# Attention scores from split operands stacked by DMA, in a causal softplus attention with a feed-forward network

## The reference

```
q, k, v = split(x @ w_qkv.T);  k_y = x @ w_ky.T           # split into 16 heads
L, L_y  = q k^T / 4,  q k_y^T / 4                          # 512 x 512 each, causal
agg = sum(exp(clip(L_y, -15, 15)) * mask) + 1e-6
w   = softplus(log(|L| + 1e-6) - log(agg + 1e-6)) * mask
out = (w / (sum(w) + 1e-6)) @ v;   x = layernorm(x + out @ w_proj.T)
h = silu(x @ w1.T * s1) * (x @ w2.T * s2)
h = gelu(h @ h1.T * s3);  h = gelu(h @ h2.T * s4);  x = layernorm(x + h @ w3.T * s5)
```

## The kernel before

| beat | after `scores_y`, early | after `sum_exps` and `scores_w`, before `sum_weights` |
|---|---|---|
| 0 | `sum_values` | `turn` (even slot) |
| 1 | `flip_sums` | `ky_proj` for the next unit |
| 2 | `spread_c` | `turn` (even), `project_out` (odd) |
| 3 | `k_proj` | |
| 4 | `flip_sums` | `q_proj` for the next unit |
| 5 | `v_proj` | `project_out` (even) |

## Time and profile before

### The profile page before, as it was taken

One profiled execution on the slowest core, in us unless ns is written; L12 is line 12 of the kernel. 1 busy time (PEld: TensorE's weight loads), 2 busy tenths in 40 slices (PEclk: granted clock), 3 DMA queues, 4 the chain that ended last, 5 costly groups with the idle time before them and its releaser, 6 DMA issues.

```text
span 1367.8 us, 22887 instructions
## 1 busy us (share of the span) xinstructions
PE 1248.2 (91%) x8214; PEld 807.9 (59%) x8214; DVE 728.6 (53%) x1232; ACT 622.8 (46%) x819; POOL 138.2 (10%) x188
## 2 busy tenths in 40 slices
PE   4888999999999999875499999999999999999996
PEld 2433444444443444433388788787887878878785
DVE  2556778686877767675343534435244352443523
ACT  3666767767677766563232313223132231322311
POOL 1212122222221122220000000000000000000000
PEclk9999999999999999998799999999999999999998
DMA  2011312222321411000640000000000000000000
GB/s 90 1 55 32 97 60 96 73 92 77 101 83 46 138 46 55 1 31 32 230 180 16 31 0 16 31 15 31 0 15 31 15 31 0 15 31 15 31 0 16
DMA packets 31942, 66.88 MB, mean 49 GB/s; under 512 B 2848, under 2 KB 8608, under 8 KB 31904
## 3 DMA queue, kind: packets, MB, share of 16 engines
q1 hardware_dynamic: 31904, 66.35, 14.3%
HBM read 46.42 MB, written 19.92 MB: 49 GB/s over the span
## 4 chain that ended last, share of the span: by engine, by line
issue 51%; POOL 0%; DVE 0%; POOLq 0%; DVEq 0%
POOL f_rstd L865 0%; DVE f_res L872 0%; POOLq L965 0%; DVEq L877 0%; POOL f_minus_half L963 0%; POOLq L83 0%
## 5 line engine op out<-in xcount | busy, mean ns | idle before, releaser
L991 ACT ACTIVATE f_h_full<-f_layer_bank,f_scales 128x512 f32<-128x512 f32 x128 | 88.0, 687 | 354.7 <-PE f_layer_bank L1105 354.6
L380 ACT ACTIVATE e_ring<-score_banks 128x1024 f32<-128x1024 f32 (+1 forms) x192 | 158.8, 879 | 134.4 <-PE score_banks L704 134.2
L541 DVE TENSOR_TENSOR w_ring<-score_banks,keep 128x1024 int32<-128x1024 int32 (+1 forms) x192 | 191.8, 1041 | 48.5 <-PE score_banks L704 47.1
L1105 PE MATMUL f_layer_bank<-f_ha_hi,f_w_all 128*128 128x512 f32 x512 | 204.4, 399 | 2.8 <-DVE f_h_full L1033 2.3
L1105 PE MATMUL f_layer_bank<-f_hb_hi,f_w_all 128*128 128x512 f32 x512 | 202.6, 396 | 0.0
L1105 PE MATMUL f_layer_bank<-f_ha_lo,f_w_all 128*128 128x512 f32 x512 | 202.5, 396 | 0.0
L1105 PE MATMUL f_layer_bank<-f_hb_lo,f_w_all 128*128 128x512 f32 x512 | 202.4, 395 | 0.0
L532 DVE TENSOR_SCALAR e_ring<-e_ring 128x2048 f32<-128x2048 f32 (+1 forms) x96 | 100.4, 1046 | 114.3 <-ACT e_ring L380 114.2
L387 ACT ACTIVATE w_ring<-w_ring 128x2048 f32<-128x2048 f32 (+1 forms) x96 | 157.2, 1637 | 6.4 <-DVE w_ring L541 6.2
L293 POOL TENSOR_SCALAR_AFFINE_SELECT e_ring<-e_ring 128x512 f32<-128x512 f32 (+1 forms) x96 | 79.3, 826 | 438.1 <-DVE e_ring L532 437.3
L1105 PEld LDWEIGHTS f_layer_bank<-f_ha_hi,f_w_all 128*128 128x128 f32 x512 | 96.1, 188 | 33.9 <-DVE f_ha_lo L1025 6.5
(11 more groups left out here) (111 smaller groups left out, 1573.5 us busy)
## 6 DMA issues: line engine op xcount, KB each, us to landing
piece<-in_wf SPq DMA_DIRECT2D x44, 256.0 KB, 2.8
wf_copy<-piece SPq DMA_DIRECT2D x44, 256.0 KB, 2.9
f_w_all<-wf_copy SPq DMA_DIRECT2D x2, 4096.0 KB, 25.1
f_x_turn<-x SPq DMA_DIRECT2D x9, 512.0 KB, 3.3
xq<-in_xt SPq DMA_DIRECT2D x8, 512.0 KB, 4.5
xv<-in_xt SPq DMA_DIRECT2D x8, 512.0 KB, 3.8
res<-in_xn SPq DMA_DIRECT2D x8, 512.0 KB, 4.4
x<-res SPq DMA_DIRECT2D x8, 512.0 KB, 2.8
```

The lines of the kernel that those rows point to most:

```text
L380: nc.scalar.activation(e_ring[:, t % RING, 2 * i:2 * i + 2, 0:cols], pair_banks(y_pair(t, i), cols), ACT.Exp).then_inc(exp_done, 1)
L541: nc.vector.tensor_tensor(w_ring[:, t % RING, 2 * i:2 * i + 2, 0:cols].bitcast(I32), pair_banks(w_pair(t, i), cols).bitcast(I32), keep[:, ...
L991: nc.scalar.activation(h_full[m % 2][:], f_bank[m % RING][:], ACT.Gelu, scale=scales[:, 1 + layer, m:m + 1]).then_inc(gelu_done, 1)
L1105: mm = nc.tensor.matmul(out, left.bitcast(dt), right.bitcast(dt), start=first and n == 0, stop=last and n == 1)
```

## The change

The two operands of each score are split into hi (rounded to fp32r) and lo (the rest, fp32r too), and are laid on 32 partitions as hi and lo of the 16 rows of one head. One fp32r matmul of (k_hi, k_lo) with (q_hi, q_lo) gives hi*hi + lo*lo; a second, with the keys' halves exchanged (`order` 1), adds lo*hi + hi*lo into the same bank.

- **Matmuls.** Each float32 matmul of the scores becomes two fp32r matmuls. The masked copies and `in_quad` go.
- **Splitting.** For each unit q, k_y, k and qc are copied whole, then rounded (hi), then subtracted (lo): q on ACT, ACT, DVE; k_y on ACT, ACT, POOL; k on ACT, ACT, POOL; qc on DVE three times. Rounding waits for the copy's own semaphore.
- **Stacking.** 24 DMAs per unit on SP, each of 64 partitions x 2 KB (128 KB) from SBUF to every second partition of a stack in SBUF: 4 for q, 8 for k_y, 8 for k, 4 for qc.
- **Order.** `q_proj` of the next unit moves from the late place of beat 4 to the early place of beat 3, `k_proj` from there to the late place of beat 4, with their copies on ACT. In SP's order `stack_qc` and `stack_ky` stand between the third and fourth piece, `stack_q` behind the fourth, `stack_k` at the slot's end; the load of `xq` moves a slot ahead (`next_x`).
- **Ring.** `e_ring` has two buffers in place of three.
- **Heads.** The set of four heads of a beat is rows 0 to 63 or 64 to 127 of the projection, in place of every second head; the indices of the sums follow.

```
+            def stack(to, place, src, g, stacked):
+                there, here = to[place:P:2, :], src[64 * g:64 * g + 64, :]
+                sp.dma_start(there.bitcast(F32), here.bitcast(F32)).then_inc(stacked, 16)
+            def stack_ky(u):
+                reach_alone(sp, ky_lo_made, u.index + 1, sp_passed)
+                reach_alone(sp, y_scores, BEATS * (u.index - 1), sp_passed)
+                for g in range(2):
+                    for order in range(2):
+                        stack(ky_stack[g][u.half][:, order, :], order, ky_hi, g, ky_stacked[g])
+                        stack(ky_stack[g][u.half][:, order, :], 1 - order, ky_lo, g, ky_stacked[g])
+            def stack_qc(v):
+                reach_alone(sp, qc_lo_made, v.index + 1, sp_passed)
+                reach_alone(sp, w_scores, BEATS * (v.index - 1), sp_passed)
+                for g in range(2):
+                    stack(qc_stack[g][v.half][:], 0, qc_hi, g, qc_stacked[g])
+                    stack(qc_stack[g][v.half][:], 1, qc_lo, g, qc_stacked[g])
...
                 if check and check != "last":
                     load_piece(k, 2, check)
+                if 3 in w:
+                    stack_qc(k.shift(-1))
+                if project:
+                    stack_ky(k.shift(1))
+                if check and check != "last":
                     load_piece(k, 3, check)
+                if project:
+                    stack_q(k.shift(1))
                 if norm is not None:
                     reach_alone(sp, ln_step, LN_STEPS * (norm + 1), sp_passed)
                     sp.dma_start(x1[norm], res[:]).then_inc(x1_stored, 16)
+                if y:
+                    stack_k(k)
...
+            def ky_rest(u):
+                reach_alone(pool, ky_hi_made, u.index + 1, pool_passed)
+                nc.gpsimd.tensor_tensor(ky_lo[:], ky_full[:], ky_hi[:].bitcast(F32), ALU.subtract).then_inc(ky_lo_made, 1)
...
             def q_keep(u):
                 reach(act, q_ready, u.index + 1)
-                reach(act, y_scores, BEATS * (u.index - 1))
-                reach(act, qc_made, 2 * (u.index - 1))
-                nc.scalar.mul(q[0][u.half][:], misc[:], in_quad[:, 0:1]).then_inc(q0_made, 1)
+                reach(act, qc_made, u.index - 1)
+                nc.scalar.mul(q_full[u.half][:], misc[:], HD ** -0.5).then_inc(q_made, 1)
+
+            def q_halve(u):
+                reach(act, q_made, u.index + 1)
+                for g in range(2):
+                    reach(act, q_stacked[g], 32 * u.index)
+                nc.scalar.copy(q_hi[:], q_full[u.half][:]).then_inc(q_hi_made, 1)
...
             def exps(k, t):
-                reach(act, e_summed, y_beat(k, t) - RING + 1)
+                reach(act, e_summed, y_beat(k, t) - E_RING + 1)
...
             def qc_make(v):
                 reach(dve, spread_ready, v.index + 1)
...
+                nc.vector.tensor_tensor(qc_full[:], misc[:], q_full[v.half][:], ALU.mult).then_inc(qc_made, 1)
                 for g in range(2):
-                    nc.vector.tensor_tensor(qc[g][v.half][:], misc[:], q[g][v.half][:], ALU.mult).then_inc(qc_made, 1)
+                    reach(dve, qc_stacked[g], 32 * v.index)
+                reach(dve, qc_made, v.index + 1)
+                nc.vector.tensor_copy(qc_hi[:], qc_full[:]).then_inc(qc_hi_made, 1)
+                reach(dve, qc_hi_made, v.index + 1)
+                nc.vector.tensor_tensor(qc_lo[:], qc_full[:], qc_hi[:].bitcast(F32), ALU.subtract).then_inc(qc_lo_made, 1)
...
                 for at, j in CHUNK_TILES[t % CHUNKS]:
-                    for r in range(QUAD):
-                        mm = nc.tensor.matmul(score[:, 2 * pair(t, r // 2) + r % 2, at:at + T - P * j],
-                                              left[lanes(r), P * j:P * j + P], right[lanes(r), P * j:T], start=True, stop=True)
+                    for order in range(2):
+                        for r in range(QUAD):
+                            mm = nc.tensor.matmul(score[:, 2 * pair(t, r // 2) + r % 2, at:at + T - P * j],
+                                                  left[lanes(r), order, P * j:P * j + P], right[lanes(r), P * j:T],
+                                                  start=order == 0, stop=order == 1)
...
             def scores_w(k, t, y):
-                reach(pe, k_made, u.index + 1)
-                reach(pe, qc_made, 2 * u.index + 2)
+                g = at // CHUNKS
+                reach(pe, k_stacked[g], 64 * (u.index + 1))
+                reach(pe, qc_stacked[g], 32 * (u.index + 1))
...
-                    if t == 3 and y:
-                        k_proj(k)
+                    if t == 3 and project:
+                        q_proj(k.shift(1))
...
-                    if t == 4 and project:
-                        q_proj(k.shift(1))
+                    if t == 4 and y:
+                        k_proj(k)
```

More of the change, by code:

```diff
@@ L202, in of_quad @@
         def of_quad(cols, g):
-            return cols.rearrange("p i (r g) -> p i r g", g=2)[:, :, :, g]
+            return cols.rearrange("p i (g r) -> p i g r", g=2)[:, :, g, :]
         ALL, NONE = (0, 1, 2, 3, 4, 5), ()
         def run(slot, fori):
-            slot(Unit(0, 0), w=NONE, before=(False, False))
+            slot(Unit(0, 0), w=NONE, before=(False, False), next_x=1)
             slot(Unit(0, 1), w=(3, 4, 5), before=(True, False), x=1)
-            slot(Unit(1, 0))
+            slot(Unit(1, 0), next_x=2)
             slot(Unit(1, 1), x=2, divide=0, check="first")
             with fori(2, BATCH - 1) as j:
-                slot(Unit(j, 0), out=j - 2, first_in_loop=True, check="mid")
+                slot(Unit(j, 0), out=j - 2, next_x=j + 1, first_in_loop=True, check="mid")
                 slot(Unit(j, 1), x=j + 1, divide=j - 1, norm=j - 2, check="mid")
@@ L249, in load_piece, with slot @@
                     sp.dma_start(wf[n - 1], piece[(s - 1) % 2][:]).then_inc(wf_copied, 16)
-            def slot(k, y=True, x=None, out=None, norm=None, check=None, **_):
+            def slot(k, y=True, project=True, w=ALL, next_x=None, out=None, norm=None, check=None, **_):
                 if y and k.half == 0:
@@ L324, in slot @@
                         mask_e(k, t)
+                    if t == 1 and project:
+                        ky_rest(k.shift(1))
+                    if t == 4 and y:
+                        k_rest(k)
                     if t == 5 and y:
                         add_values(k)
+            ky_rest(Unit(0, 0))
             run(slot, pool.Fori)
@@ L463, in slot @@
                         turn_keep(out, 1)
[L464 to L465 removed]
+                    if t == 4 and y:
+                        k_keep(k)
                     if t < STEPS and check and (check != "first" or t > 0) and (check != "last" or t == 0):
@@ L619, in slot @@
                         keep_agg(k, 0)
+                    if t == 4 and project:
+                        q_rest(k.shift(1))
                     if y:
@@ L719, in scores_w, with sum_keys @@
                 u, at = weights_of(k, t)
-                reach(pe, k_made, u.index + 1)
-                reach(pe, qc_made, 2 * u.index + 2)
+                g = at // CHUNKS
+                reach(pe, k_stacked[g], 64 * (u.index + 1))
+                reach(pe, qc_stacked[g], 32 * (u.index + 1))
                 reach(pe, abs_done, 2 * m)
                 reach(pe, exp_done, 2 * n + 1 if y else BEATS * UNITS * 2)
-                scores(t, w_pair, key[u.half], qc[at // CHUNKS][u.half]).then_inc(w_scores, 1)
-            def sum_keys(t, ring, stationary, first, last):
+                scores(t, w_pair, k_stack[g][u.half], qc_stack[g][u.half]).then_inc(w_scores, 1)
+            def sum_keys(t, at_ring, ring, stationary, first, last):
                 for at, j in CHUNK_TILES[t % CHUNKS]:
                     for r in range(QUAD):
-                        mm = nc.tensor.matmul(acc[lanes(r), P * j:T], stationary(j, r), ring[:, t % RING, r, at:at + T - P * j],
+                        mm = nc.tensor.matmul(acc[lanes(r), P * j:T], stationary(j, r), ring[:, at_ring, r, at:at + T - P * j],
                                               start=first and t % CHUNKS == 0, stop=last and t % CHUNKS == CHUNKS - 1)
```

135 lines of the change are left out of this document (80 added, 55 removed).

## The result

| | before | after |
|---|---|---|
| median of 5 runs | 1370.33 us (1369.60 to 1373.92) | 1361.87 us (1358.96 to 1364.01) |
| profiled execution | 1369.58 us | 1364.01 us |
| its granted TensorE clock, mean | 0.986 | 0.964 |

The ratio is 0.9932 (0.9921 to 0.9943): 8.5 us faster, where 33.0 were predicted, and above the range of 1314 to 1359. Between the two profiled executions the gain is 5.6 us, so 27.4 of the 33.0 are missing there.

What follows compares the result with a forecast made beforehand. PE's order was taken to set most beats, with loops through ACT and DVE close behind. From 1369.6 us, 33.0 saved over slot pairs, ends and start, plus 0.7, gave 1337.3; own range 1324 to 1350, with rivals 1314 to 1359.

Steps and rivals of the forecast that it cites:

- Slots 2 to 15: The loop's seven slot pairs: 4.7 us saved per pair, less 0.2 per slot for exposed roundings.
- Start: Before the first scores: 4.7 us later, first two score groups save 0.8 each, net 3.1 lost; slots 0, 1 save 1.5, 2.0.
- Tail: Last stretch, where only weight scores run: nine `scores_w` save 2.5 us.
- POOL's subtractions hold DVE: Rival, 8%: each of two GpSimd subtractions costs DVE 0.5 us on the deciding path, 14 us return: 1351.
- Beat 2 of the even slot: Even slot's beat of 4.84 us: `logs` already holds `sum_weights`, so only 0.15 us saved.
- The readers of PSUM decide: Rival, 12%: emptying PSUM sets the beats, each slot saves only one `scores_y` per two beats, 0.9 us: 1357.
- PE's work decides everywhere: Rival, 10%: nothing of ACT or DVE shows, all PE work saved counts, 61 us with the ends: 1309.
- fp32r on 32 partitions is not faster: Rival, 6%: score matmuls save nothing, the start costs 4.7 us and beat 3 0.65 a slot: 1384, or 1378.
- qc lands late: Rival, 8%: `scores_w` of beats 3 in 15 slots waits; each us of landing beyond 3.9 costs 15: 1384.
- PE waits for `qc_stack`: Sign of a wrong forecast: no PE wait for a DMA was expected ahead of `scores_w`.
- The ring of two: Two buffers of exponentials: costs nothing, as PE's order already has `sum_exps` of beat t-2 ahead of `scores_y`.
- The rounding between `exps` and `logs`: ACT in beat 3: q's copy and rounding end `logs` 0.65 us later; exposed roundings charged 0.2 per slot.

Runs made afterwards that it cites:

- run 2: Changed kernel with unread filler matmuls at the start, ahead of `sum_weights` in some beats of the slots, and in the tail: 1355.5 us, ratio 0.9899 to the kernel before.
- run 5: Filler of run 2 on the changed kernel, thinned in the tail and slot 1 to where there is room: 1351.57 us, ratio 0.9862 to the kernel before.
- run 9: Run 5 with k_y's subtraction moved from GpSimd to DVE, q's rounding behind `logs`, and slot 1's filler only in beat 3: 1344.01 us, ratio 0.9819.
- run 3: Changed kernel with each pair of fp32r score matmuls replaced by one float32 matmul, splits, stacks, DMAs and orders kept: 1381.32 us, ratio 1.0085 to the kernel before.
- run 6: Run 5 with GpSimd's two subtractions cut to 4 of 512 columns: 1345.33 us, ratio 0.9818 to the kernel before.
- run 8: Changed kernel, without filler, with the second matmul of each score pair left out: 1354.41 us, ratio 0.9874 to the kernel before.
- run 4: Kernel before with two buffers of exponentials in place of three, nothing else: 1369.09 us, ratio 0.9997.
- run 7: Run 5 with ACT's rounding of q moved behind `logs` in beat 3: 1349.87 us, ratio 0.9854 to the kernel before.
- run 10: Changed kernel without filler, with k_y's subtraction moved from GpSimd to DVE and q's rounding behind `logs`: 1351.13 us, ratio 0.9848 to the kernel before.
- Run 1: Changed kernel with filler at the start only, 12 matmuls before and 8 behind the first scores: 1360.39 us, ratio 0.9921 to the kernel before.

## Why the prediction was wrong, and where it was right

**The step that failed is the sum's silent assumption** that each duration of before holds after, at the clock of the windows shown, 1.00. The terms took PE's work away and left it waiting for `logs` and `absolute`. The clock was in no term and no rival, and the sum put it at nothing without a reason; the runs showed about 10 us of it in slots 2 to 15 alone (runs 2 and 5). The Trainium skill says (TensorE: Matmul & The Clock Gate, What's actually happening) that half clock is the default, from which activity releases the engine, and (A second HAM failure mode: psum-queue depth-cycling) that frequent small idle times between groups of matmuls can be enough for it to fall back. The trace agrees in that the fall at 340 us came after an idle time of 1.48 us, though slot 7 kept its clock after 1.49.

- *Slots 2 to 15* gained 17.2 of 30.1 us. With filler and no half clock the same slots gain 27.5 (run 2), so the clock took 10.3 of the 12.9 missing. The even slots' beat 2 (below) took 4.1 in five slots, and other beats gave 1.5 more than the sum had.
- *Start.* The first scores came at 25.74 us, 4.95 later where 4.7 was predicted. The terms behind that failed: slots 0 and 1 were to save 5.1 us with the first groups, and cost 2.2. Slot 0 stayed at 24.48 us and slot 1 went from 30.24 to 32.40, both at half clock in part. With filler they took 22.42 and 30.59 (run 2), and 21.86 and 29.02 in run 9, so at best 3.8 of the 5.1 were there to be had.
- *Tail.* 2.5 us were to be saved and 4.5 were lost. The windows of the changed kernel over its weight scores show a clock of 0.76, where before it was 1.00:

```profile
586.46:625.17 38.71, 28.99 (x241) 13.53 (x237) 24.75 (x30) 18.95 (x20) 3.38 (x6) 0.76 0.22 55
```

```profile
596.00:631.00 35.00, 25.17 (x244) 10.46 (x236) 24.10 (x29) 19.27 (x20) 3.80 (x6) 1.00 0.07 25
```

Filler there brought 0.91 and 58.05 us (run 5); no run had a tail at full clock. The clock is not all of it: PE waited 1.7 us for `qc_stack` in the tail, and with float32 scores (run 3) the tail took 59.3 us too, at a clock of 0.86.

Together the filler shows 16.6 of the 27.4 us as the clock's: 10.3 in slots 2 to 15, 3.9 in slots 0 and 1, and 2.4 in the tail of run 5. The even slots' beat 2 is 4.1. The other 6.7 are 8.2 at the start and in the tail, less the 1.5 of the other beats; how the 8.2 divide is not shown.

**The rivals.** *POOL's subtractions hold DVE* was right as a mechanism, at 6.2 us (run 6) and not 14: in most beats the subtraction meets nothing that decides. It took 1.28 us where 1.0 was assumed. Beat 2 of the even slot, predicted at 4.69 us, took 5.51, and this makes up the 0.8 us between the predicted 34.4 and 35.18; without the subtractions it took 4.83 (run 6). The rule of the Trainium skill (SBUF — State Buffer, two separate sides: the port pair is held for a whole instruction, and the other engine waits) agrees: beside a subtraction 11 of the 44 compares took 0.96 to 1.46 us for 0.69, and 5 of the 32 normalisations 1367 to 1502 ns for 406. *The readers of PSUM decide*, at 1357, came nearest by its number and not by its mechanism: float32 scores would then have cost little beside the changed kernel, and cost about 20 us (run 3), and filler would not have helped. The rule of the Trainium skill (TensorEngine Tiling (Array Packing), PSUM Bottleneck) is not seen to decide here: PE's wait for `absolute`, which empties PSUM, fell from 18.2 to 10.9 us, and what grew, from 24.4 to 44.9, is its wait for `logs`, which reads SBUF. *PE's work decides everywhere* falls with run 8: half the score matmuls, 7.5 us, and even at full clock beat 0 of an even slot lost 0.24 us (5.18 to 4.94) for two rounds of 0.24 fewer. *fp32r on 32 partitions is not faster* falls: the 512 group is busy 0.74 us for 1.14, the mixed 0.85 for 1.15, the 256 group 0.51 for 0.71; 0.40, 0.30 and 0.20 saved, nearly as predicted. The rival *qc lands late* was wrong in its size and right in its place. Two views of the changed kernel:

```profile
PE score_banks L782 <- DMA ky_stack<-ky_lo: 7.4, 1, 7.4
PE acc_bank L810 <- ACT w_ring L471: 44.9, 38, 1.8
```

```profile
DMA to landing us min/median/max: 2.2/2.4/3.4
```

The first fence is of its waits by pairs (in all, times, longest), the second of the transfers to `qc_stack`. The wait for `ky_stack` is the start's single one. The landing took 2.4 us in the middle where 2.9 was taken, and in all PE waited 3.1 us for `qc_stack`, in 3 times: 0.5 in slot 6, 0.9 in slot 10 and 1.7 in the tail. "PE waits for `qc_stack`" was one of the prediction's own signs of being wrong. The longer one of the loop:

```profile
392.22 0.74 PE L782 MATMUL score_banks<-qc_stack,k_stack 32*128 32x512 f32 x8 [0.91 <-DMA qc_stack<-qc_lo]
```

The cover was used up in the even slots 4 to 12: the second stack landed 8.2 to 9.2 us after beat 2's start (7.0 predicted), and `scores_w` began 0.12 to 0.15 us behind it, though only slots 6 and 10 show a wait of 0.5 us or more. In slot 8 `qc_lo` was done at 4.25 us and not 3.4, as the slow compare stands ahead of it, its second issue went out at 5.15 and not 4.1, and landing took 3.3. In slot 10 SP came to it 1.0 us after `qc_lo` was done, with its third piece ahead.

The wait for `logs` is the kind that the fall at 340 us came behind: 44.9 us in 38 times.

**Smaller terms.** The ring of two costs nothing, as said (run 4). The rounding between `exps` and `logs` was charged 0.2 a slot with 0.65 inside beat 3; beat 3 took 5.59 as predicted, and a late rounding gave back 0.15 with filler (run 7) and about 0.4 without (run 10, with the subtraction moved too). SP's issues of `qc_stack` took about 0.55 us (0.46 to 0.92) and not 0.4, which is part of its late landing. Three sums of the prediction don't come out of their terms. The start's add up to 5.0 and not 4.7, and 4.95 was measured. ACT's copies in beat 3 add 0.74 and not 0.65. And the slots of 34.4 and 36.1 leave out the 0.2 for rounding that the sum has; with it they are 34.6 and 36.3.

**What stays open.** Slot 7 has the same instructions and the same 1.49 us of idle time as slot 9 and kept its clock. Run 1, whose slots from 2 on have the same instructions as the changed kernel's, kept its clock in slot 2 (33.68 us for 35.11) and lost it in slot 13 (36.91 for 36.04). The mean clock orders the executions of the changed kernel only roughly. What exactly decides was not found; that less work between the same waits brings more falls is shown by runs 3, 2 and 8 together: in slots 2 to 15 half clock took 0 us with float32 scores, 31 with the change, 65 with half its matmuls, and 0 with filler. How much a tail at full clock would take is open too.

## What to carry to other kernels

When a change shortens TensorE's groups and not its waits, put the clock into the sum: list the idle times that grow, and count as a bound that the time around them runs at 1.2 GHz. Afterwards compare two slots with the same instructions before any other explanation, and look at the clock of windows of one slot, since a page's slices round it away. Then idle time may be filled with matmuls that nobody reads, only where TensorE waits anyway, and fitted again whenever a change shortens that wait (run 7). A new GpSimd operation on large tiles is looked for in the longest durations of VectorE's instructions, which stand beside their medians. A transfer with little cover, as `qc_stack` here, is looked for in TensorE's waits after every change.

## What had not been expected of the hardware

- TensorE fell to 1.2 GHz for 3 to 7 us after an idle time of 1.5 us, in a stretch where it was busy for 32 of 37 us. A slot of the loop with such a stretch took 1.4 to 1.5 us more (slot 10 took 1.7, of which 0.3 belongs to a wait for `qc_stack`).
- More work made the program quicker: run 2's PE is busy 34.32 us in an odd slot, against 32.27, and the slot takes 36.20 for 37.48.
- DVE's two-input operation on 512 columns went from 0.68 to up to 1.46 us beside a GpSimd subtraction of 1.28 us.
- An issue of 128 KB between two places of SBUF, 64 partitions to every second one, landed in 2.2 to 3.4 us even with the DMA share at 0.77.
